# Order of a recurrent stage: transposes in one group, up-projections side by side, feature copies moved to ScalarE

## The chip, the cores and the metric

The kernel runs on one core of one Trainium2 chip. The metric is the device time of one execution, in microseconds; three runs gave 3738.53 us as their median (3736.28 to 3739.94). Five engines work side by side, each through its own list of instructions in a fixed order: TensorE (PE; its weight loads are shown as PEld), VectorE (DVE), ScalarE (ACT), GpSimd (POOL) and SyncE (SP), which issues the DMAs. They meet only at semaphores.

## What is computed

A decoder block over 32 sequences of 256 tokens with 256 features: four sLSTM layers (the first stage), then cross attention and a quantised feed-forward (the second stage, which the change does not touch). One sLSTM layer, cut to what matters:

```python
xc = silu(causal_conv(xn, 4 taps) + cb)             # xn = layernorm(x)
gi, gf = xc @ wi, xc @ wf;  gz, go = xn @ wz, xn @ wo   # per head, 64 x 64
def step(h, c, n, m):                               # 256 tokens, one after another
    ir, fr, zr, og = wx_t + h @ rk + b
    lfm = m + log_sigmoid(fr);  mn = maximum(ir, lfm)
    ig, fg = exp(ir - mn), exp(lfm - mn)
    cn = fg*c + ig*tanh(zr);  nn = fg*n + ig
    hn = sigmoid(og) * cn / nn
x = x + layernorm_per_head(h) * gn_w
x = x + (gelu(u[:336]) * u[336:]) @ wd              # u = layernorm(x) @ wu
```

## The kernel before

The first stage runs 279 steps (`STEPS`). A step handles one token of all 32 sequences in each of the four layers at once: partition group l (32 partitions) holds layer l, six steps behind layer l - 1, so a step is one token through the recurrence, with convolution, norms and feed-forward of neighbouring tokens beside it. Each engine has a loop over j written out by hand in one fixed order; nothing else sets the order.

On TensorE three shapes of the array take turns: full 128x128 transposes (L260, L308), products with 64 rows and 32 columns (`add_bias` L278, `by_head` L269, `centred` L288), and products with 112 or 128 rows and 32 columns (`feed_up` L295, `feed_down` L302). A step goes: transposes of `xm` ("after_cell") and `xn` ("normed"), bias, z and o gates, first half of up, transposes of `h` and `hid`, i and f gates, recurrence, `centred`, `feed_down`, second half of up.

The recurrence closes through the other engines: after the recurrent product (`rec_done`) ScalarE takes Exp and Ln of the f gates (L378, L380), loads another table (L381), and takes tanh of the gates o and z (L383, L384) and of half the decay logit (`td`, L357). VectorE makes `v` (L535), `sf` (L537), and from these the decay logit `dl` (L478: both inputs lie in SBUF), then the cell in four operations (L483, L487, L492, L471) up to `h`, which TensorE transposes. Of VectorE's operations three read both inputs from SBUF: `dl`, the convolved features `xst` (L503) and the residual `xm` (L540). The others read one from PSUM ("banks") or have only one.

GpSimd makes the convolution from `xnt`, the normed features that ScalarE copies out of PSUM (L348): products of taps 2 and 3 in one 128x512 operation (L565), their sum (L571), the products of taps 1 and 0 (L565), the sums that give `part[0]` and `part[1]` (L578, `conv_done`), and the last sum (L579). All of them read SBUF only. ScalarE takes tanh of `part[0]` (`ct`, L365).

Of the kernel before, what the change touches and what calls it, by code (L numbers as in the profile page):

```python
# [14 lines left out]
P = 128  # L15
# [85 lines left out]
def slstm(nc, ctx, a, x4, pieces):  # L101
# [102 lines left out]
    def heads_of(ap, n):  # L204
        return ap.rearrange("p (r n d) -> p n r d", n=HALF, d=DH)[:, n]

    def reach(engine, semaphore, count):
        if count > 0:
            engine.wait_ge(semaphore, count)

# [12 lines left out]
    with nc.Block() as block:  # L223
# [33 lines left out]
        def _(pe):  # L257
# [48 lines left out]
            def hidden_features():  # L306
                for i in range(UTILES):
                    mm = nc.tensor.transpose(bank[0:UT, CV, i * P:(i + 1) * P], hid[:, i * UT:(i + 1) * UT], ident[:])  # L308
                return mm
# [10 lines left out]
            pe.wait_ge(bias_moved, 2 * DMA)  # L320
            add_bias(1).then_inc(first_gates, 1)
# [24 lines left out]
        def _(act):  # L346
            def copy(dst, src):
                return nc.scalar.activation(dst, src, ACT.Copy)  # L348

            def both(ap):  # L350
                return ap.rearrange("p n t -> p (n t)")
# [3 lines left out]
            for j in range(STEPS):  # L355
                act.wait_ge(d_ready, j + 1)
                nc.scalar.activation(td[:], dl[:], ACT.Tanh, scale=-0.5).then_inc(td_done, 1)  # L357
                reach(act, yn_done, j)
                reach(act, rstd_done, j)
                nc.scalar.activation(gl[:], bank[:, UPG, 0:UP], ACT.Gelu, scale=rs2).then_inc(gelu_done, 1)  # L360
                act.wait_ge(xnt_ready, j + 1)
                copy(both(xmt[:]), bank[:, CV, D:]).then_inc(xmt_copied, 1)
                copy(both(xnt[:, j % NRING]), bank[:, CV, 0:D]).then_inc(xnt_copied, 1)
                act.wait_ge(conv_done, j + 1)
                nc.scalar.activation(ct[:], part[:, j % 2, 0], ACT.Tanh).then_inc(ct_done, 1)  # L365
                nc.scalar.preload_act_table_set(LOG_EXP)  # L366
                nc.scalar.activation(spb[:], dl[:], ACT.Exp).then_inc(growth_exp, 1)
                act.wait_ge(growth_exp, j + 1)
                act.wait_ge(h_done, HALF * (j + 1))
                nc.scalar.activation(gate(j - 1, 1), heads(spb[:]), ACT.Ln, bias=1.0).then_inc(growth_log, 1)  # L370
                act.wait_ge(hidt_ready, j + 1)
                copy(both(hidt[:]), bank[0:UT, CV, 0:UTILES * P]).then_inc(hidt_copied, 1)
# [5 lines left out]
                nc.scalar.activation(heads(fb[:]), gate(j, 1), ACT.Exp).then_inc(f_exp, 1)  # L378
                act.wait_ge(f_exp, j + 1)
                nc.scalar.activation(fb[:], fb[:], ACT.Ln, bias=1.0).then_inc(f_log, 1)  # L380
                nc.scalar.preload_act_table(ACT.Gelu)  # L381
                act.wait_ge(sf_done, j + 1)
                nc.scalar.activation(gate(j, 3), gate(j, 3), ACT.Tanh, scale=0.5).then_inc(o_done, 1)  # L383
                nc.scalar.activation(gate(j, 2), gate(j, 2), ACT.Tanh).then_inc(z_done, 1)  # L384
            act.wait_ge(z_done, STEPS)

        @block.vector
        def _(dve):
            n = 0
            for buf, val in ((xr, 0.0), (h, 0.0), (half_r, 0.0), (ls, NEVER), (dl, 0.0), (xm, 0.0), (xst, 0.0), (prod, 0.0), (hid, 0.0),  # L390
                             (hidt, 0.0), (xnt, 0.0), (xmt, 0.0), (gl, 0.0), (xn, 0.0), (v, 0.0), (sf, 0.0), (rstd, 0.0), (eps, EPS), (bias, 0.0), (pick16, 0.0),
# [4 lines left out]
            for l in range(LAYERS):  # L396
                nc.vector.memset(begun[group(l), 0:LAG * l + LEAD + 1], 0.0).then_inc(w_step, 1)
                nc.vector.memset(never[group(l), 0:LAG * l + LEAD + 1], NEVER).then_inc(w_step, 1)
                n += 2
            dve.wait_ge(w_step, n)  # L400
# [69 lines left out]
            def ratio_to_h(j, n):  # L470
                return nc.vector.scalar_tensor_tensor(out=h[:, n * P:(n + 1) * P].rearrange("p (r d) -> p r d", r=2),  # L471
                                                      in0=gates_of(j - 1)[:, :, n, 3, :], scalar=1.0, in1=heads_of(half_r[:], n),
                                                      op0=ALU.add, op1=ALU.mult)

            for j in range(STEPS):
                cell = gate(j - 1, 2)
                reach(dve, sf_done, j)
                nc.vector.scalar_tensor_tensor(out=dl[:], in0=v[:], scalar=-60.0, in1=sf[:], op0=ALU.max,  # L478
                                               op1=ALU.subtract).then_inc(d_ready, 1)
                reach(dve, xm_done, j)  # L480
                nc.vector.bn_stats(stat2[:], xm[:, (j - 1) % MRING]).then_inc(ln2_stat, 1)
                reach(dve, z_done, j)
# [6 lines left out]
                dve.wait_ge(ln2_stat, j + 1)  # L489
# [6 lines left out]
                ratio_to_h(j, 0).then_inc(h_done, 1)  # L496
                dve.wait_ge(gelu_done, j + 1)
                reach(dve, up_done, j)
                nc.vector.scalar_tensor_tensor(out=hid[:], in0=bank[:, UPV, 0:UP], scalar=rs2, in1=gl[:], op0=ALU.mult,
                                               op1=ALU.mult).then_inc(hid_done, 1)  # L500
                ratio_to_h(j, 1).then_inc(h_done, 1)
# [6 lines left out]
                dve.wait_ge(ht_ready, j + 1)  # L508
                nc.vector.tensor_scalar(ht[:].rearrange("p n t -> p (n t)"), bank[:, FD, D:], 1.0 / H_SCALE, None,  # L509
                                        ALU.mult).then_inc(ht_copied, 1)  # L510
# [3 lines left out]
                dve.wait_ge(ln1_stat, j + 1)  # L514
                nc.vector.bn_aggr(mv1, stat1[:]).then_inc(ln1_mv, 1)
                dve.wait_ge(growth_log, j + 1)
                nc.vector.scalar_tensor_tensor(out=heads(sp[:]), in0=gate(j - 1, 1), scalar=40.0, in1=heads(dl[:]), op0=ALU.min,
                                               op1=ALU.max).then_inc(grown, 1)
                dve.wait_ge(grown, j + 1)
                if j < STARTED:  # L520
# [8 lines left out]
                nc.vector.tensor_tensor(yn[:].rearrange("p (r n d) -> p r n d", r=2, n=HALF),  # L529
                                        bank[:, UPG:UPG + 2, UP:UP + P].rearrange("p r (n d) -> p r n d", n=HALF),  # L530
                                        rs.rearrange("p (n r) -> p r n", n=HALF)[:, :, :, None].broadcast_to(
                                            [P, 2, HALF, DH]), ALU.mult).then_inc(yn_done, 1)
                dve.wait_ge(f_exp, j + 1)
                dve.wait_ge(ls_done, j + 1)
                nc.vector.tensor_tensor(heads(v[:]), heads(ls[:]), gate(j, 0), ALU.subtract).then_inc(v_done, 1)  # L535
# [3 lines left out]
                dve.wait_ge(yn_done, j + 1)  # L539
                nc.vector.tensor_tensor(xm[:, j % MRING], yn[:], xr[:, (j - 3) % XRING, :], ALU.add).then_inc(xm_done, 1)  # L540
# [992 lines left out]
```

## Time and profile before

| | us |
|---|---|
| median of three runs | 3738.53 |
| profiled execution | 3732.63 |
| its span (first to last instruction) | 3730.9 |
| PE busy | 3615.0 (97%) |
| DVE busy | 3460.5 (93%) |
| ACT busy | 3064.7 (82%) |
| POOL busy | 2253.7 (60%) |
| mean granted TensorE clock | 0.990 of full speed |

The first stage takes from about 51 us to 2214 us of the span, the second the rest. In a timeline, a row is a run of like instructions: its start, its length from the first start to the last end, and how many. On each engine the next instruction can start somewhat before the one in front has ended, so the difference of two starts is what a row costs its engine, and the length is what somebody has to wait who needs the result.

### The profile page before, as it was taken

Reading aid. Unit: us, or ns where it says so; the run is one execution under the profiler, and the core shown is the slowest. Engines: PE = TensorE matmul, PEld = TensorE weight load, DVE = VectorE, ACT = ScalarE, POOL = GpSimd, SP = SyncE. Lnnn points to the kernel's source line nnn. Section 1 sums busy time; section 2 is a strip of 40 time slices with the busy share of each in tenths; the row PEclk is TensorE's granted clock in tenths of the full one; section 3 lists DMA queues with packets and bytes.
Section 4 is the critical chain, followed back from the end, with each engine's and each line's share of the span. In section 5 each row is a group of like instructions: output and inputs, shape, how many; then the busy total and the mean of one; then the engine's idle time right before and its main releaser. Section 6 shows DMA issues by size and latency. Waiting matters only on the chain. (4 is left out here: it accounts for less than half of the span.)

```text
span 3730.9 us, 167466 instructions
## 1 busy us (share of the span) xinstructions
PE 3615.0 (97%) x71481; PEld 2282.1 (61%) x71481; DVE 3460.5 (93%) x9241; ACT 3064.7 (82%) x6357; POOL 2253.7 (60%) x2395
## 2 busy tenths in 40 slices
PE   6999999999999999999999987999999999999997
PEld 3666666665666666666666654666666666666664
DVE  8999999999999999999999987889988898888886
ACT  4999999999999999999999984677776677777675
POOL 3777777777777777777777764444444444444442
PEclk9999999999999999999999998999999999999998
DMA  2000221000000000000000000000000000100000
GB/s 82 25 25 25 56 59 53 25 25 25 25 25 25 25 25 25 25 25 25 25 25 25 25 26 18 24 24 24 24 24 24 24 24 28 32 24 24 24 16 10
DMA packets 99973, 104.27 MB, mean 28 GB/s; under 512 B 17297, under 2 KB 95005, under 8 KB 98729
## 3 DMA queue, kind: packets, MB, share of 16 engines
q1 hardware_dynamic: 99224, 93.56, 8.7%
q8 instruction: 560, 9.18, 1.0%
q14 instruction: 189, 1.54, 0.1%
HBM read 48.52 MB, written 17.53 MB: 18 GB/s over the span
## 5 line engine op out<-in xcount | busy, mean ns | idle before, releaser
L565 POOL TENSOR_TENSOR conv_products<-normed_features,conv_taps_by_token 128x256 f32<-128x256 f32 (+1 forms) x837 | 757.9, 919 | 530.2 <-ACT normed_features L348 530.1
L771 POOL TENSOR_TENSOR exps_of_both_halves<-scores 128x256 f32<-128x256 f32 x512 | 424.2, 851 | 583.8 <-ACT scores L1027 578.4
L295 PE MATMUL banks<-up_centred,after_cell_features 128*32 128x336 f32 x8928 | 740.3, 449 | 1.1 <-ACT after_cell_features L348 0.5
L295 PEld LDWEIGHTS banks<-up_centred,after_cell_features 128*32 128x32 f32 x8928 | 260.5, 109 | 277.6 <-issue 224.1
L302 PE MATMUL banks<-down,hidden_features 112*32 112x256 f32 x6696 | 419.2, 383 | 0.0
L578 POOL TENSOR_TENSOR conv_partial_sums<-conv_products,conv_partial_sums 128x512 f32<-128x512 f32 x279 | 370.5, 1328 | 21.9
L1027 ACT ACTIVATE scores<-scores 128x512 f32<-128x512 f32 x512 | 305.4, 626 | 77.7 <-DVE scores L1175 74.0
L366 ACT ACT_TABLE_LOAD x279 | 358.0, 1283 | 5.2
L381 ACT ACT_TABLE_LOAD x279 | 358.0, 1283 | 5.1
L1175 DVE SCALAR_TENSOR_TENSOR scores<-banks,score_top 128x512 f32<-128x512 f32 x512 | 327.9, 681 | 26.1 <-PE banks L857 25.5
L269 PE MATMUL banks<-recurrent_weights,h_features 64*32 64x256 f32 x8928 | 313.1, 379 | 0.3 <-DVE h_features L509 0.2
L867 PE MATMUL banks<-scores,v_tokens 128*32 128x256 f32 x4096 | 274.0, 385 | 11.9 <-ACT scores L1027 11.7
L579 POOL TENSOR_TENSOR conv_partial_sums<-conv_products,conv_partial_sums 128x256 f32<-128x256 f32 x279 | 265.1, 950 | 0.0
L302 PEld LDWEIGHTS banks<-down,hidden_features 112*32 112x32 f32 x6696 | 189.0, 109 | 121.3
L571 POOL TENSOR_TENSOR conv_partial_sums<-conv_products,conv_partial_sums 128x256 f32<-128x256 f32 x279 | 220.3, 790 | 65.9 <-DVEq L466 44.0
L835 PE MATMUL banks<-batch_inputs_hi,qkv_weights_hi 128*128 128x256 f16 x1024 | 196.0, 273 | 11.3 <-POOL batch_inputs_lo L759 9.8
L269 PEld LDWEIGHTS banks<-recurrent_weights,h_features 64*32 64x32 f32 x8928 | 196.1, 106 | 8.3 <-DVE h_features L509 1.5
L835 PE MATMUL banks<-batch_inputs_lo,qkv_weights_hi 128*128 128x256 f16 x1024 | 196.0, 273 | 0.0
L835 PE MATMUL banks<-batch_inputs_hi,qkv_weights_lo 128*128 128x256 f16 x1024 | 195.9, 273 | 0.0
L867 PEld LDWEIGHTS banks<-scores,v_tokens 128*32 128x32 f32 x4096 | 120.9, 110 | 107.6 <-ACT scores L1027 27.1
L269 PE MATMUL banks<-gate_weights,convolved_features 64*32 64x128 f32 x8928 | 186.2, 275 | 0.0
L503 DVE SCALAR_TENSOR_TENSOR convolved_features<-tanh_half_conv,conv_partial_sums 128x256 f32<-128x256 f32 x279 | 180.0, 645 | 0.5 <-ACT tanh_half_conv L365 0.5
(222 smaller groups left out, 9933.3 us busy)
## 6 DMA issues: line engine op xcount, KB each, us to landing
layer_inputs<-layer_outputs SPq DMA_DIRECT2D x279, 96.0 KB, 2.0
layer_inputs<-in_x SPq DMA_DIRECT2D x280, 32.0 KB, 1.8
x_scratch<-layer_outputs SPq DMA_DIRECT2D x279, 32.0 KB
x_tokens<-in_x SPq DMA_DIRECT2D x32, 256.0 KB, 3.0
context_features<-in_ctx SPq DMA_DIRECT2D x32, 256.0 KB, 3.7
layers_out<-x_scratch SPq DMA_DIRECT2D x32, 256.0 KB, 2.8
out<-result SPq DMA_DIRECT2D x64, 128.0 KB, 1.8
up_centred<-in_ff_up SPq DMA_DIRECT2D x1, 2688.0 KB
```

What stands on the lines that cost most here:

```text
L269: mm = nc.tensor.matmul(bank[group(l), 2 * (j % 2) + odd, at + g0 * DH:at + g1 * DH], src[r, n, group(l)], w[r, l, n, g0:g1, :].rearrange( ...
L295: mm = nc.tensor.matmul(bank[group(l), b, 0:UP], xmt[:, n, group(l)], up[:, l, n, at:at + UP], start=n == 0, stop=n == HALF - 1, skip_grou ...
L302: mm = nc.tensor.matmul(bank[group(l), FD, 0:D], hidt[:, i, group(l)], down[:, l, i, :], start=i == 0, stop=i == UTILES - 1, skip_group_ch ...
L366: nc.scalar.preload_act_table_set(LOG_EXP)
L381: nc.scalar.preload_act_table(ACT.Gelu)
L565: return nc.gpsimd.tensor_tensor(prod[:, i:i + n], xnt[:, j % NRING].rearrange("p n t -> p (n t)")[:, None, :].broadcast_to([P, n, HALF * ...
L578: nc.gpsimd.tensor_tensor(new[:, 0:2], prod[:, 0:2], old[:, 1:3], ALU.add).then_inc(conv_done, 1)
L771: nc.gpsimd.tensor_tensor(psum[:, i % RING, :], pr[:, i % RING, 0:S], pr[:, i % RING, S:2 * S], ALU.add).then_inc(halves_added, 1)
L835: mm = nc.tensor.matmul(bank[:, b, i * S:(i + 1) * S], w_[:, m, h, (2 * n + i) * P:(2 * n + i + 1) * P], x_[:, j % SLOTS, src, h, :], star ...
L867: mm = nc.tensor.matmul(bank[32 * g:32 * g + 32, b, at:at + S], stationary(kt, i), pr[:, i % RING, kt * S:(kt + 1) * S], start=kt == 0, st ...
L1027: nc.scalar.activation(pr[:, i % RING, :], pr[:, i % RING, :], ACT.Exp, scale=S_SCALE).then_inc(exp_done, 1)
L1175: nc.vector.scalar_tensor_tensor(out=pr[:, i % RING, :].rearrange("p (k s) -> p k s", k=KT), in0=bank[:, i % SCORES, :].rearrange("p (k s) ...
```

## The change

TensorE's step becomes: transposes of `xn`, `h`, `xm` and `hid` together; i and f gates, recurrence, `centred`; `feed_down`, both halves of up; then bias and z and o gates of the next step. The transposed `hid` goes into the i and f places of the gate banks of the step before, and the growth logs, which stood there, into the transposed `h`'s place in the bank of `feed_down`. The copy of the transposed `h` moves from VectorE (L509) to ScalarE, behind the second table load; the copies of `xn` and `xm` and all tanh operations move within ScalarE's step. On VectorE the scaling by the norm and the residual become four 128x64 operations that read PSUM and write `xm`; `sf` now comes ahead of `v`, and `dl` behind the layer's output `xo`. On GpSimd the products of taps 2 and 3 move from the head of a step to behind `conv_done`.

```diff
@@ tensor, in the loop over j
-                reach(pe, xm_done, j)
-                transposes(CV, D, xm[:, (j - 1) % MRING], xmt_ready)
                 transposes(CV, 0, xn, xnt_ready)
-                add_bias(j)
-                by_head(j, wg, xnt[:, (j - 1) % NRING], 2, GATES)
-                pe.wait_ge(xmt_copied, j + 1)
-                feed_up(UPG, 0).then_inc(g_done, 1)
                 pe.wait_ge(h_done, HALF * (j + 1))
                 transposes(FD, D, h, ht_ready)
-                pe.wait_ge(xnt_copied, j + 1)
-                hidden_features().then_inc(hidt_ready, 1)
+                transposes(CV, D, xm[:, (j - 1) % MRING], xmt_ready)
+                pe.wait_ge(hid_done, j + 1)
+                hidden_features(j - 1).then_inc(hidt_ready, 1)
                 ...
+                pe.wait_ge(grown, j + 1)
                 feed_down().then_inc(down_done, 1)
-                pe.wait_ge(yn_done, j + 1)
+                pe.wait_ge(xmt_copied, j + 1)
+                pe.wait_ge(xm_done, j + 1)
+                feed_up(UPG, 0).then_inc(g_done, 1)
                 feed_up(UPV, UP).then_inc(up_done, 1)
+                pe.wait_ge(ls_done, j + 1)
+                add_bias(j + 1)
+                pe.wait_ge(xnt_copied, j + 1)
+                by_head(j + 1, wg, xnt[:, j % NRING], 2, GATES)
@@ scalar, in the loop over j
+                copy(both(ht[:]), bank[:, FD, D:], 1.0 / H_SCALE).then_inc(ht_copied, 1)
...
-                nc.scalar.activation(gate(j - 1, 1), heads(spb[:]), ACT.Ln, bias=1.0).then_inc(growth_log, 1)
+                nc.scalar.activation(bank[:, FD, D:], spb[:], ACT.Ln, bias=1.0).then_inc(growth_log, 1)
@@ vector, in the loop over j
-                nc.vector.tensor_scalar(ht[:].rearrange("p n t -> p (n t)"), bank[:, FD, D:], 1.0 / H_SCALE, None,
-                                        ALU.mult).then_inc(ht_copied, 1)
...
-                nc.vector.tensor_tensor(yn[:].rearrange(...), bank[:, UPG:UPG + 2, UP:UP + P].rearrange(...), rs..., ALU.mult).then_inc(yn_done, 1)
-                nc.vector.tensor_tensor(xm[:, j % MRING], yn[:], xr[:, (j - 3) % XRING, :], ALU.add).then_inc(xm_done, 1)
+                for r in range(2):
+                    for n in range(HALF):
+                        at = slice(r * P + n * DH, r * P + n * DH + DH)
+                        add = nc.vector.scalar_tensor_tensor(out=xm[:, j % MRING, at], in0=bank[:, UPG + r, UP + n * DH:UP + n * DH + DH],
+                                                             scalar=rs[:, 2 * n + r:2 * n + r + 1], in1=xr[:, (j - 3) % XRING, at],
+                                                             op0=ALU.mult, op1=ALU.add)
+                add.then_inc(xm_done, 1)
@@ gpsimd, in the loop over j
-                reach(pool, taps_rest, j)
-                nc.gpsimd.tensor_tensor(new[:, 3], prod[:, 3], new[:, 4], ALU.add).then_inc(sum3_done, 1)
                 reach(pool, xnt_copied, j)
                 reach(pool, conv_done, j)
+                products(0, 1, j - 1).then_inc(taps_first, 1)
                 products(1, 1, j - 1).then_inc(taps_second, 1)
-                products(0, 1, j - 1).then_inc(taps_first, 1)
                 ...
                 nc.gpsimd.tensor_tensor(new[:, 0:2], prod[:, 0:2], old[:, 1:3], ALU.add).then_inc(conv_done, 1)
+                products(2, 2, j - 1).then_inc(taps_rest, 1)
+                pool.wait_ge(taps_rest, j + 1)
+                nc.gpsimd.tensor_tensor(new[:, 3], prod[:, 3], new[:, 4], ALU.add).then_inc(sum3_done, 1)
                 nc.gpsimd.tensor_tensor(new[:, 2], prod[:, 2], old[:, 3], ALU.add).then_inc(sum2_done, 1)
-                pool.wait_ge(xnt_copied, j + 1)
-                pool.wait_ge(sum2_done, j + 1)
-                products(2, 2, j).then_inc(taps_rest, 1)
```

GpSimd's row, one step of the first stage, before; "conv_products" are products with the taps, "conv_partial_sums" the sums of them, and L578 is the one that gives `conv_done`:

```order
L565 TENSOR_TENSOR conv_products<-normed_features,conv_taps_by_token 128x512 [waits sum_of_third_tap,normed_copied]
L571 TENSOR_TENSOR conv_partial_sums<-conv_products,conv_partial_sums 128x256 [waits other_taps_done]
L565 TENSOR_TENSOR conv_products<-normed_features,conv_taps_by_token 128x256 [waits conv_done,normed_copied]
L565 TENSOR_TENSOR conv_products<-normed_features,conv_taps_by_token 128x256
L578 TENSOR_TENSOR conv_partial_sums<-conv_products,conv_partial_sums 128x512 [waits sum_of_third_tap,first_tap_done]
L579 TENSOR_TENSOR conv_partial_sums<-conv_products,conv_partial_sums 128x256
```

The same step after the change, from the wait for ScalarE's copy on (L583 gives `conv_done`):

```order
L572 TENSOR_TENSOR conv_products<-normed_features,conv_taps_by_token 128x256 [waits conv_done,normed_copied]
L572 TENSOR_TENSOR conv_products<-normed_features,conv_taps_by_token 128x256
L583 TENSOR_TENSOR conv_partial_sums<-conv_products,conv_partial_sums 128x512 [waits second_tap_done,sum_of_third_tap]
L572 TENSOR_TENSOR conv_products<-normed_features,conv_taps_by_token 128x512
L586 TENSOR_TENSOR conv_partial_sums<-conv_products,conv_partial_sums 128x256 [waits other_taps_done]
L587 TENSOR_TENSOR conv_partial_sums<-conv_products,conv_partial_sums 128x256
```

The same six operations, but the 128x512 product has gone from first place to fourth.

VectorE's row before, from `sf` (L537) over `dl` (L478) to `h` (L471):

```order
L537 SCALAR_TENSOR_TENSOR softplus_of_minus_f<-softplus_logs,banks 128x256 [waits f_log]
L540 TENSOR_TENSOR after_cell<-cell_out,layer_inputs 128x256 [waits yn_done]
L544 TENSOR_TENSOR layer_outputs<-banks,after_cell 128x256 [waits x4_stored,layer_inputs_moved,down_done]
L478 SCALAR_TENSOR_TENSOR minus_decay_logit<-log_normaliser_minus_i,softplus_of_minus_f 128x256 [waits softplus_done]
L481 BN_STATS bn_stats_ln2<-after_cell 128x6 [waits after_cell_done]
L483 SCALAR_TENSOR_TENSOR banks<-half_cell_ratio,banks 128x4x64 [waits tanh_z_done]
```

And after the change, the same stretch:

```order
L534 SCALAR_TENSOR_TENSOR after_cell<-banks,rstd,layer_inputs 128x64 [waits centred_ready]
L534 SCALAR_TENSOR_TENSOR after_cell<-banks,rstd,layer_inputs 128x64 x3
L539 SCALAR_TENSOR_TENSOR softplus_of_minus_f<-softplus_logs,banks 128x256 [waits f_log]
L542 TENSOR_TENSOR log_normaliser_minus_i<-log_normaliser,banks 128x256 [waits normaliser_done]
L546 TENSOR_TENSOR layer_outputs<-banks,after_cell 128x256 [waits x4_stored,layer_inputs_moved,down_done]
L548 SCALAR_TENSOR_TENSOR minus_decay_logit<-log_normaliser_minus_i,softplus_of_minus_f 128x256 [waits minus_i_done]
L551 BN_STATS bn_stats_ln2<-after_cell 128x6 [waits after_cell_done]
L485 SCALAR_TENSOR_TENSOR banks<-half_cell_ratio,banks 128x4x64 [waits tanh_z_done]
```

`xm` is now written from PSUM in four pieces ahead of `sf`; `dl` (L548) still comes right behind `xo` and ahead of the statistics and of the cell's first operation.

## Rows read from the trace of the kernel before

**Rows 1.** Busy time by engine in a stretch: start:end, length, PE, PEld, DVE, ACT, POOL, clock, DMA share, GB/s.

```profile
1000.00:1400.00 400.00, 399.81 (x10377) 247.84 (x10384) 389.05 (x1187) 378.51 (x826) 294.19 (x310) 1.00 0.10 25
```

**Rows 2.** Timeline of TensorE, one step: start us, length us, engine, line, operation, operands, count.

```profile
1000.02 0.41 PE L278 MATMUL banks<-bias_parts,layer_of_row 64*32 64x512 f16 x8
1000.82 1.34 PE L295 MATMUL banks<-up_centred,after_cell_features 128*32 128x336 f32 x16
1002.08 0.44 PE L260 MATMUL banks<-identity,h 128*128 128x128 f32 x2
...
1007.19 0.44 PE L260 MATMUL banks<-identity,after_cell 128*128 128x128 f32 x2
1007.77 0.41 PE L278 MATMUL banks<-bias_parts,layer_of_row 64*32 64x512 f16 x8
```

**Rows 3.** Timeline of TensorE in a narrow window: the last four of that run of sixteen.

```profile
1001.69 0.47 PE L295 MATMUL banks<-up_centred,after_cell_features 128*32 128x336 f32 x4
```

**Rows 4.** Two VectorE lines over the first stage: duration minimum/median/maximum, first and last start.

```profile
L503 DVE SCALAR_TENSOR_TENSOR convolved_features<-tanh_half_conv,conv_partial_sums x279: 415/664/669, 50.5 to 2212.6; 128x256 f32<-128x256 f32 x140
```
```profile
L540 DVE TENSOR_TENSOR after_cell<-cell_out,layer_inputs x278: 411/418/994, 55.4 to 2208.8; 128x256 f32<-128x256 f32 x139
```

**Rows 5.** Timeline of GpSimd, one step.

```profile
1000.86 1.29 POOL L565 TENSOR_TENSOR conv_products<-normed_features,conv_taps_by_token 128x512 f32<-128x512 f32 x1 [1.87 <-ACT normed_features L348]
...
1002.99 1.42 POOL L565 TENSOR_TENSOR conv_products<-normed_features,conv_taps_by_token 128x256 f32<-128x256 f32 x2
1004.49 1.33 POOL L578 TENSOR_TENSOR conv_partial_sums<-conv_products,conv_partial_sums 128x512 f32<-128x512 f32 x1
1005.78 0.96 POOL L579 TENSOR_TENSOR conv_partial_sums<-conv_products,conv_partial_sums 128x256 f32<-128x256 f32 x1
```

**Rows 6.** Timeline of VectorE, the same step.

```profile
1001.77 0.66 DVE L503 SCALAR_TENSOR_TENSOR convolved_features<-tanh_half_conv,conv_partial_sums 128x256 f32<-128x256 f32 x1
...
1005.73 0.42 DVE L540 TENSOR_TENSOR after_cell<-cell_out,layer_inputs 128x256 f32<-128x256 f32 x1
...
1006.53 0.49 DVE L478 SCALAR_TENSOR_TENSOR minus_decay_logit<-log_normaliser_minus_i,softplus_of_minus_f 128x256 f32<-128x256 f32 x1
1006.95 0.41 DVE L481 BATCH_NORM_STATS2 bn_stats_ln<-after_cell 128x6 f32<-128x256 f32 x1
1007.29 0.40 DVE L483 SCALAR_TENSOR_TENSOR banks<-half_cell_ratio,banks 128x256 f32<-128x256 f32 x1
...
1008.64 0.29 DVE L471 SCALAR_TENSOR_TENSOR h<-banks,half_cell_ratio 128x128 f32<-128x128 f32 x1
```

**Rows 7.** Timelines of GpSimd and VectorE in another step.

```profile
1109.41 1.29 POOL L565 TENSOR_TENSOR conv_products<-normed_features,conv_taps_by_token 128x512 f32<-128x512 f32 x1 [1.88 <-ACT normed_features L348]
```
```profile
1110.56 0.42 DVE L503 SCALAR_TENSOR_TENSOR convolved_features<-tanh_half_conv,conv_partial_sums 128x256 f32<-128x256 f32 x1
```

**Rows 8.** Timeline of ScalarE, from the end of the recurrent product on.

```profile
1004.42 0.38 ACT L378 ACTIVATE softplus_logs<-banks 128x256 f32<-128x256 f32 x1 [0.26 <-PE banks L269]
...
1006.56 0.37 ACT L383 ACTIVATE banks<-banks 128x256 f32<-128x256 f32 x1
1006.84 0.36 ACT L384 ACTIVATE banks<-banks 128x256 f32<-128x256 f32 x1
1007.11 0.42 ACT L357 ACTIVATE tanh_half_d<-minus_decay_logit 128x256 f32<-128x256 f32 x1
1007.41 0.54 ACT L360 ACTIVATE gelu_of_gate<-banks,rstd 128x336 f32<-128x336 f32 x1
...
1008.16 0.38 ACT L348 ACTIVATE normed_features<-banks 128x256 f32<-128x256 f32 x1
1008.42 0.42 ACT L365 ACTIVATE tanh_half_conv<-conv_partial_sums 128x256 f32<-128x256 f32 x1
1008.86 1.28 ACT L366 ACT_TABLE_LOAD   x1
1010.16 0.42 ACT L367 ACTIVATE growth_logs<-minus_decay_logit 128x256 f32<-128x256 f32 x1
```

More of the change, by code:

```diff
@@ L346, in _, with copy @@
         def _(act):
-            def copy(dst, src):
-                return nc.scalar.activation(dst, src, ACT.Copy)
+            def copy(dst, src, scale=1.0):
+                return nc.scalar.activation(dst, src, ACT.Copy, scale=scale)
             def both(ap):
@@ L355, in _ @@
             for j in range(STEPS):
[L356 removed]
+                reach(act, v_done, j)
+                nc.scalar.activation(gate(j - 1, 3), gate(j - 1, 3), ACT.Tanh, scale=0.5).then_inc(o_done, 1)
+                nc.scalar.activation(gate(j - 1, 2), gate(j - 1, 2), ACT.Tanh).then_inc(z_done, 1)
+                reach(act, d_ready, j)
                 nc.scalar.activation(td[:], dl[:], ACT.Tanh, scale=-0.5).then_inc(td_done, 1)
[L358 removed]
+                act.wait_ge(conv_done, j + 1)
+                nc.scalar.activation(ct[:], part[:, j % 2, 0], ACT.Tanh).then_inc(ct_done, 1)
+                reach(act, g_done, j)
                 reach(act, rstd_done, j)
                 nc.scalar.activation(gl[:], bank[:, UPG, 0:UP], ACT.Gelu, scale=rs2).then_inc(gelu_done, 1)
[L361 to L365, printed above, removed]
                 nc.scalar.preload_act_table_set(LOG_EXP)
                 nc.scalar.activation(spb[:], dl[:], ACT.Exp).then_inc(growth_exp, 1)
+                act.wait_ge(ht_ready, j + 1)
+                copy(both(ht[:]), bank[:, FD, D:], 1.0 / H_SCALE).then_inc(ht_copied, 1)
+                act.wait_ge(xmt_ready, j + 1)
+                copy(both(xnt[:, j % NRING]), bank[:, CV, 0:D]).then_inc(xnt_copied, 1)
                 act.wait_ge(growth_exp, j + 1)
[L369 to L370 removed]
+                act.wait_ge(ht_copied, j + 1)
+                nc.scalar.activation(bank[:, FD, D:], spb[:], ACT.Ln, bias=1.0).then_inc(growth_log, 1)
                 act.wait_ge(hidt_ready, j + 1)
[L372 removed]
+                copy(hidt[:], hidden_of(j - 1)).then_inc(hidt_copied, 1)
+                act.wait_ge(gn_stat, HALF * (j + 1))
                 act.wait_ge(ln1_mv, j + 1)
@@ L378, in _ @@
                 nc.scalar.activation(heads(fb[:]), gate(j, 1), ACT.Exp).then_inc(f_exp, 1)
+                copy(both(xmt[:]), bank[:, CV, D:]).then_inc(xmt_copied, 1)
                 act.wait_ge(f_exp, j + 1)
@@ L399, in _ @@
                 n += 2
+            nc.vector.bn_stats(stat2[:], xm[:, 0]).then_inc(w_step, 1)
+            n += 1
             dve.wait_ge(w_step, n)
@@ L468, in _ @@
             dve.wait_ge(first_x, DMA)
[L470 to L473, printed above, removed]
             for j in range(STEPS):
                 cell = gate(j - 1, 2)
[L477 to L482, printed above, removed]
+                dve.wait_ge(z_done, j + 1)
                 nc.vector.scalar_tensor_tensor(out=cell, in0=heads(half_r[:]), scalar=-2.0 / H_SCALE, in1=cell, op0=ALU.mult,
@@ L495, in _ @@
                 dve.wait_ge(ratio_done, j + 1)
-                ratio_to_h(j, 0).then_inc(h_done, 1)
+                for n in range(HALF):
+                    nc.vector.scalar_tensor_tensor(out=h[:, n * P:(n + 1) * P].rearrange("p (r d) -> p r d", r=2),
+                                                   in0=gates_of(j - 1)[:, :, n, 3, :], scalar=1.0, in1=heads_of(half_r[:], n),
+                                                   op0=ALU.add, op1=ALU.mult).then_inc(h_done, 1)
+                reach(dve, up_done, j)
                 dve.wait_ge(gelu_done, j + 1)
-                reach(dve, up_done, j)
                 nc.vector.scalar_tensor_tensor(out=hid[:], in0=bank[:, UPV, 0:UP], scalar=rs2, in1=gl[:], op0=ALU.mult,
                                                op1=ALU.mult).then_inc(hid_done, 1)
-                ratio_to_h(j, 1).then_inc(h_done, 1)
                 dve.wait_ge(ct_done, j + 1)
@@ L528, in _ @@
                 dve.wait_ge(cen_ready, j + 1)
[L529 to L535, printed above, removed]
+                for r in range(2):
+                    for n in range(HALF):
+                        at = slice(r * P + n * DH, r * P + n * DH + DH)
[3 more added lines that the diff above has]
+                add.then_inc(xm_done, 1)
                 dve.wait_ge(f_log, j + 1)
```

42 lines of the change are left out of this document (25 added, 17 removed).

## The prediction

> **What bounds the kernel now.** First I look at the busy time by engine in a stretch of the first stage [rows 1]: of 400 us TensorE is busy 399.8, VectorE 389, ScalarE 378.5, GpSimd 294. All of the first three are nearly full, so the order of waits decides as much as the work. Next TensorE's timeline [rows 2]: from bias to bias 7.75 us pass, and no row there shows idle time. Its transposes do not wait for their inputs: those of xm start at 1007.19, and xm was finished at 1006.15 [rows 2, 6]. What they wait for is the array: the transposes of h start 0.39 us after the last four up matmuls, while four such matmuls inside the run take 0.29 (0.87 us for the first twelve) [rows 2, 3]. So the step before is TensorE's own loop of 7.75 us. By the first and last start of one line the first stage lies between 50.5 and 2212.6 us [rows 4]: 2162.1 over 278 steps is 7.777 a step, so outside this loop there are only 0.025 a step, 7 us in all. The second stage is the same code before and after; I add nothing for it.
>
> **A stall that has no row of its own.** The third view is the duration of VectorE's operations that have both inputs in SBUF. The convolved features, L503, take 664 ns in the middle and 415 at the least [rows 4]. The timelines show why. The slow one starts at 1001.77 with GpSimd's 128x512 product running until 1002.15 (1000.86 + 1.29), and ends at 1002.43, 0.28 behind the product's end [rows 5, 6]. In the step where only 0.14 us of the product are left (it ends at 1110.70), L503 starting at 1110.56 takes 0.42 [rows 7]. The decay logit dl, L478, does the same: it starts at 1006.53, GpSimd's L579 ends at 1006.74, and dl ends at 1007.02, again 0.28 later [rows 5, 6]. L540 starts 0.09 ahead of L578's end and takes 0.42. One rule fits all: such an operation, started while GpSimd works, ends at its own 0.41 or at GpSimd's end plus 0.28, whichever is later. Before the change this hits xst, where TensorE has other work, and dl by 0.08. The question is where it hits afterwards.
>
> The Trainium skill (SBUF — State Buffer, Who interferes with whom) says that a VectorE instruction with two SBUF inputs contends with a GpSimd instruction that reads SBUF, and that the later one blocks fully. The trace agrees that it waits for the whole GpSimd instruction, but not that all its work is still ahead of it then: 0.28 us follow, not 0.41. By the page the sum below would be 0.13 us a step higher, 36 us in all.
>
> **The change part by part.**
>
> TensorE: the products and transposes are as many as before. Of six switches between shapes of the array four are left, and a switch costs what the end of the up run costs over its inside, 0.39 - 0.29 = 0.10 us [rows 2, 3]. So the loop falls by 0.2 us to 7.55; ends of 0 (the neighbours now behind one another don't overlap better) and 0.4 (each twice as dear).
>
> VectorE loses the copy of h and two 128x256 operations and gets four of 128x64. No row has that form: each costs between 0.10 and the 0.29 of a 128x128 one [rows 6], I take 0.14. They stand ahead of sf, which waits for ScalarE's Ln and hides them at 0.14; at 0.29 each they would start dl some 0.4 later, which the paragraph on dl shows to be free too (it has 0.73). xst becomes free of the stall, since in its new place GpSimd is idle; TensorE comes to the i and f gates later than xst ends either way, so that is worth nothing in the ring below.
>
> ScalarE gets one more 0.38 us copy, of h; it counts in the ring below. The copy of xm goes between Exp and Ln of f: Ln then starts two starts of 0.28 behind Exp instead of 0.38 and a latency, 0.15 later, which counts in the first rival only.
>
> The added waits on TensorE: feed_down waits for the growth, and both halves of up, bias and gates are queued behind it. With E as the end of dl (below), the growth's Ln follows the copy of xn at about E + 3.4 and the growth is done at E + 4.2, feed_down is reached past E + 5; the wait is covered by 0.8 us, and without that cover would cost one for one. The transposes of hid wait for hid, E + 2.6, and are reached at E + 2.7, a cover of 0.1. SyncE's DMAs hang on xo, which keeps its place behind feed_down.
>
> GpSimd: the products of taps 2 and 3 move from the front of its step to behind conv_done. That is the edit on which the sum rests. GpSimd's step starts when ScalarE has copied the normed features; call that moment C. I follow from rows: 0.07 to the first product (the copy at 1008.16 ends 1008.54, the product one step on from 1000.86 starts at 1008.61), 1.50 for two products and the pause behind them (1002.99 to 1004.49), 1.29 for the conv sum (1004.49 to 1005.78) [rows 5, 8]. So the 128x512 product starts at C + 2.86 and runs to C + 4.15.
>
> Now dl. Let E be its end. The chain behind it on VectorE: the statistics start 0.07 ahead of E (1006.95 against 1007.02), the cell's first operation 0.34 later, h's first half 1.35 after that, the second 0.21 later (0.29 less the overlap of 0.08), its end 0.29 on, and 0.04 to TensorE: E + 2.16 [rows 6]. From there to Exp of f, which waits for the recurrent product, 2.34 us pass before (1002.08 to 1004.42) [rows 2, 8]; the transposes of xm are now between, 0.27, so Exp of f is at E + 4.77. dl comes 2.11 behind Exp of f (1006.53 against 1004.42) and still will: xo ahead of it waits for feed_down, and those runs follow the recurrent product as before. So dl is ready to start at E + 6.88.
>
> And C: ScalarE takes td 0.04 after E (ends 0 and 0.09, what lies between dl's end and td now), then ct 0.30 later and Gelu 0.31 later (a 0.42 us tanh holds the engine 0.30: 1007.11 to 1007.41), the table load 0.56 later (0.54 and 0.02, as between ct and its load), Exp of the growth 1.29 later (1008.86 to 1010.16), the copy of h 0.30 later, that of xn 0.28 later (as from o to z), and 0.38 for it [rows 8]. Sum: 3.46. So C = E + 3.46, the product runs from E + 6.32 to E + 7.61, and dl, ready at E + 6.88, comes 0.56 behind its start and 0.73 ahead of its end. By the rule dl ends at E + 7.61 + 0.28 = E + 7.89.
>
> This is a ring: dl, td, ct, Gelu, table load, copies, four GpSimd operations, dl. It closes at **7.89 us** a step, and it feeds itself, since a later dl moves the copy and with it the product that blocks the next dl. Nothing on it is waited for from elsewhere: the transposed h is there at E + 2.65 (2.16, 0.44 and a latency) and wanted at E + 2.80; conv_done comes at C + 2.9, which is ahead of E, and ct asks behind E. TensorE's loop of 7.55 has 0.34 of idle time inside it.
>
> Sum: 7.89 - 7.75 = 0.14 us a step, times 279: +39 us. Against this L540, which by its maximum of 994 ns was sometimes blocked for a whole GpSimd operation more [rows 4], becomes an operation that reads PSUM; of the 7 us beyond the loop I take half as due to it, 4 us (ends 0 and 7). +35 us. Own time of the profiled execution 3732.6 (span 3730.9): 3768. The runs' median lies 5.9 above that execution: **3774 us**.
>
> **The rivals.**
>
> *The stall does not reach dl, and the change pays* (0.12). If the rule is another (say, only behind this product's own start of step), TensorE's 7.55 loop bounds. The second loop is shorter: from Exp of f to o 2.14 and the 0.15 above, z and its end 0.28 + 0.36 [rows 8], the cell 0.04 + 1.35 + 0.21 + 0.29 + 0.04, and 2.61 to the next Exp of f: 7.47. That is -0.20 a step, -56 us: 3683. For it: fewer switches. Against it: three kinds of VectorE operation obey the rule, and one of them is dl itself. The Trainium skill (TensorEngine Tiling (Array Packing), Key Properties) says that a change of tiling mode drains the array, which speaks for the gain on TensorE; the rows give 0.10 for one such change.
>
> *dl does all its work behind the product* (0.06): where it started long before the product's end, its own 0.41 would follow instead of 0.28. The ring becomes 8.02, +0.13 a step, 36 us more: 3810. For it speaks only that no row shows dl behind this very product; against it that L503 does the same behind it with 0.28 [rows 5, 6]. The Trainium skill's rule above (SBUF — State Buffer, Who interferes with whom) is this rival.
>
> *No change* (0.06): the product is over when dl comes, or nearly. The ring then must be 0.14 shorter than I add up, some seven of its terms 0.02 too long, or dl later by 0.6. Time 3735.
>
> *Slower by much* (0.02): dl loses against the next sum too, as L540 sometimes did, by 0.994 - 0.418 = 0.58 more a step [rows 4]: +161 us, 3935. Behind the product the next sum waits for it, so VectorE comes first.
>
> **How the numbers follow.** The forecast has 0.74. Its own range: the latencies (0.04 down, 0.05 up) and the overlaps, 0.07 us in all, is 20 us either way, 3754 to 3794. The range takes in a little on the side of no change and nearly all of the second rival: 3748 to 3808. Left out are the gain (0.12), the large loss (0.02) and some edges. What can be told from no change here is 0.2%, 7.5 us. Slower has 0.74 + 0.06 + 0.02 = 0.82, the same 0.06, faster 0.12.
>
> **What would show it.** In the profile of the changed kernel L548 (dl) should take about 1.0 us (7.89 - 6.88) and end 0.28 behind the 128x512 product of L572; L507 (xst) about 0.42. ScalarE should wait for dl ahead of td, some 0.3 us a step, and TensorE for h ahead of its transposes, about as much; TensorE's busy share in the first stage falls by a few per cent. If dl takes 0.41 to 0.5 and TensorE never waits, the first rival holds. If ScalarE waits for the transposed h, the ring I add up isn't the one that closes.

## The result, and the profile after

The changed kernel takes 3776.32 us in the median of four runs (3774.36 to 3777.15) against 3737.69 before: a ratio of 1.0102, with an interval of 1.0085 to 1.012. It is slower, as forecast, and 3776 stands against 3774. The span of the profiled execution grows from 3730.9 to 3775.4 us. One execution of experiment 3 took 8926.32 us, with the matmuls of the up projection at 1019 ns in the mean against 448 (experiment 8); no comparison uses it, and why it was slow is not known.

Two lines over the first stage of the changed kernel, dl and xst (duration minimum/median/maximum in ns, first and last start):

```profile
L548 DVE SCALAR_TENSOR_TENSOR minus_decay_logit<-log_normaliser_minus_i,softplus_of_minus_f x279: 415/1050/1068, 57.3 to 2258.9; 128x256 f32<-128x256 f32 x140
```
```profile
L507 DVE SCALAR_TENSOR_TENSOR convolved_features<-tanh_half_conv,conv_partial_sums x279: 411/414/856, 50.7 to 2254.5; 128x256 f32<-128x256 f32 x140
```

The stall has changed places: xst has gone from 664 to 414 ns, dl from 0.49 us [rows 4, 6] to 1.05. From 50.7 to 2254.5 are 2203.8 us against 2162.1, so 41.7 of the 44.5 us lie in the first stage.

GpSimd's timeline of the changed kernel, and VectorE's and ScalarE's beside it, answer to [rows 5, 6, 8]:

```profile
1004.59 1.43 POOL L572 TENSOR_TENSOR conv_products<-normed_features,conv_taps_by_token 128x256 f32<-128x256 f32 x2 [2.26 <-ACT normed_features L355]
1006.16 1.28 POOL L583 TENSOR_TENSOR conv_partial_sums<-conv_products,conv_partial_sums 128x512 f32<-128x512 f32 x1
1007.41 1.28 POOL L572 TENSOR_TENSOR conv_products<-normed_features,conv_taps_by_token 128x512 f32<-128x512 f32 x1
```
```profile
1005.66 0.51 DVE L528 TENSOR_SCALAR normed<-layer_inputs,moments,rstd 128x256 f32<-128x256 f32 x1
1006.11 0.86 DVE L534 SCALAR_TENSOR_TENSOR after_cell<-banks,rstd,layer_inputs 128x64 f32<-128x64 f32 x4
...
1007.91 1.06 DVE L548 SCALAR_TENSOR_TENSOR minus_decay_logit<-log_normaliser_minus_i,softplus_of_minus_f 128x256 f32<-128x256 f32 x1
```
```profile
1001.08 0.42 ACT L367 ACTIVATE tanh_half_d<-minus_decay_logit 128x256 f32<-128x256 f32 x1 [0.28 <-DVE minus_decay_logit L548]
1001.40 0.40 ACT L369 ACTIVATE tanh_half_conv<-conv_partial_sums 128x256 f32<-128x256 f32 x1
1001.71 0.52 ACT L372 ACTIVATE gelu_of_gate<-banks,rstd 128x336 f32<-128x336 f32 x1
1002.25 1.28 ACT L373 ACT_TABLE_LOAD   x1
1003.55 0.42 ACT L374 ACTIVATE growth_logs<-minus_decay_logit 128x256 f32<-128x256 f32 x1
1003.87 0.36 ACT L355 ACTIVATE h_features<-banks 128x256 f32<-128x256 f32 x1
1004.13 0.37 ACT L355 ACTIVATE normed_features<-banks 128x256 f32<-128x256 f32 x1
...
1009.00 0.42 ACT L367 ACTIVATE tanh_half_d<-minus_decay_logit 128x256 f32<-128x256 f32 x1 [0.29 <-DVE minus_decay_logit L548]
```

The whole ring stands here. td starts at 1001.08; the copy of xn ends at 1004.50; GpSimd's products start 0.09 later, the sum at 1006.16, the 128x512 product at 1007.41, until 1008.69. dl has started 0.50 behind that product and ends at 1008.97, 0.28 behind its end. td follows at 1009.00, 7.92 us after the one before.

Who waited for whom in 400 us of the changed kernel (us in total, times, longest):

```profile
PEld banks L264 <- DVE h L499: 22.4, 51, 0.5
ACT tanh_half_d L367 <- DVE minus_decay_logit L548: 14.4, 51, 0.3
```

Both once a step, 0.44 and 0.28 us. TensorE's busy time in such a stretch falls from 399.8 us [rows 1] to 389.7:

```profile
1000.00:1400.00 400.00, 389.70 (x10127) 246.92 (x10119) 391.82 (x1212) 372.39 (x859) 274.42 (x303) 1.00 0.09 25
```

### The profile page after: what moved, and what is told of

Same layout as the page of the kernel before. It is cut to its first block and busy times, and to the rows that moved or that the text cites. A ratio compares the mean times of both kernels' runs of the same rounds, so it can differ in the third digit from the quotient of the medians.

```text
span 3775.4 us, 168598 instructions
## 1 busy us (share of the span) xinstructions
PE 3605.5 (95%) x71489; PEld 2312.7 (61%) x71489; DVE 3514.7 (93%) x9520; ACT 3072.2 (81%) x6636; POOL 2180.0 (58%) x2395
## 5 line engine op out<-in xcount | busy, mean ns | idle before, releaser
L299 PE MATMUL banks<-up_centred,after_cell_features 128*32 128x336 f32 x8928 | 682.7, 446 | 0.0
L299 PEld LDWEIGHTS banks<-up_centred,after_cell_features 128*32 128x32 f32 x8928 | 293.2, 109 | 301.0 <-issue 248.3
L583 POOL TENSOR_TENSOR conv_partial_sums<-conv_products,conv_partial_sums 128x512 f32<-128x512 f32 x279 | 359.0, 1287 | 39.9
L548 DVE SCALAR_TENSOR_TENSOR minus_decay_logit<-log_normaliser_minus_i,softplus_of_minus_f 128x256 f32<-128x256 f32 x279 | 290.8, 1042 | 0.0
L534 DVE SCALAR_TENSOR_TENSOR after_cell<-banks,rstd,layer_inputs 128x64 f32<-128x64 f32 x1116 | 239.9, 278 | 1.8 <-PE banks L292 1.4
L586 POOL TENSOR_TENSOR conv_partial_sums<-conv_products,conv_partial_sums 128x256 f32<-128x256 f32 x279 | 222.1, 796 | 21.9
L587 POOL TENSOR_TENSOR conv_partial_sums<-conv_products,conv_partial_sums 128x256 f32<-128x256 f32 x279 | 203.1, 728 | 0.0
```

What stands on the lines that cost most here:

```text
L299: mm = nc.tensor.matmul(bank[group(l), b, 0:UP], xmt[:, n, group(l)], up[:, l, n, at:at + UP], start=n == 0, stop=n == HALF - 1, skip_grou ...
L583: nc.gpsimd.tensor_tensor(new[:, 0:2], prod[:, 0:2], old[:, 1:3], ALU.add).then_inc(conv_done, 1)
```

## Experiments

Each ratio is to the kernel before on the same chip: 3733.68 us for experiments 1 to 4, 3736.81 for 5, 7 and 8, 3731.92 for 9 and 10. "The changed kernel" is the 3776 us above; it did not run again on these chips, so differences to it, and between experiments of different chips, are uncertain by some 6 us. "The middle step" is the median distance of two starts of `L528` (`L526` in the kernel before), "the mean step" the distance of its first and last start over 278. Number 6, sf in PSUM in the kernel before, gave no measurement.

**1. dl reads one input from PSUM.** Edits: sf is written behind `down_done` to the free half of `feed_down`'s bank, in the order v, statistics, sf, xo, dl; ScalarE's tanh of the gate o waits for sf instead of v.

```diff
-                nc.vector.scalar_tensor_tensor(out=heads(sf[:]), ...).then_inc(sf_done, 1)
+                dve.wait_ge(down_done, j + 1)
+                nc.vector.scalar_tensor_tensor(out=heads(bank[:, FD, D:]), ...).then_inc(sf_done, 1)
 ...
-                nc.vector.scalar_tensor_tensor(out=dl[:], in0=v[:], scalar=-60.0, in1=sf[:], op0=ALU.max,
+                nc.vector.scalar_tensor_tensor(out=dl[:], in0=v[:], scalar=-60.0, in1=bank[:, FD, D:], op0=ALU.max,
```

> The changed kernel, with sf written to the free half of feed_down's bank (PSUM) instead of SBUF, so that dl reads only one input from SBUF; sf waits for feed_down, so sf, xo, dl follow in this order and v and the statistics come ahead. Theory (the ring through GpSimd, 7.92 us a step): dl takes 0.41 instead of 1.05 whatever GpSimd does, the ring is open, and TensorE's loop of about 7.55 bounds: 0.37 x 279 = 103 us less than the changed kernel, about 3675, under the kernel before too. Rival (the step is long because TensorE's new order or ScalarE's extra copy is, and dl only fills idle time): no gain, 3770 to 3780.

Measured: 3688.13 us, ratio 0.9876 (0.9861 to 0.9891). dl takes 409 ns at the median and 416 at most, with GpSimd's order as in the changed kernel. It runs inside the 128x512 product and is not blocked:

```profile
1006.70 1.29 POOL L573 TENSOR_TENSOR conv_products<-normed_features,conv_taps_by_token 128x512 f32<-128x512 f32 x1
```
```profile
1007.48 0.41 DVE L551 SCALAR_TENSOR_TENSOR minus_decay_logit<-log_normaliser_minus_i,banks 128x256 f32<-128x256 f32 x1
```

The step is 7.54 us in the middle, as expected, but 7.61 in the mean, and the time 13 us above the expected 3675. `L528` takes up to 1526 ns in this run; experiments 5 and 10 ask how much of the loss is due to it.

**2. The product waits for dl.** The cleanest test: one wait on the engine that has idle time.

```diff
+                reach(pool, d_ready, j)
                 products(2, 2, j - 1).then_inc(taps_rest, 1)
```

> The changed kernel, with one wait more on GpSimd: the 128x512 product starts only when dl is done. No operation, place or operand of another engine is changed. Theory: dl takes 0.41; the three GpSimd operations behind it then run until about 2.9 us after dl, so that xst is blocked for some 0.25 us and TensorE waits about 0.1 for it: 7.55 to 7.65 a step, 3675 to 3702. Rival (GpSimd's work is what is long, or GpSimd is idle 2.3 us a step and so cannot matter): the same as the changed kernel, or slower by the delay of its sums.

Measured: 3671.14 us, ratio 0.9828 (0.9811 to 0.9844). dl in its timeline lines:

```profile
L548 DVE SCALAR_TENSOR_TENSOR minus_decay_logit<-log_normaliser_minus_i,softplus_of_minus_f x279: 406/415/418, 56.9 to 2156.2; 128x256 f32<-128x256 f32 x140
```

A wait added to GpSimd takes 105 us off the changed kernel, and no operation was changed. The four executions spread more than elsewhere (3660.02 to 3674.11). The middle step is 7.47, below the 7.55 to 7.65 expected, and the time is below the 3675 to 3702: TensorE's loop was put too long, and xst takes 463 ns at the median, 0.05 more than in the changed kernel where 0.25 was expected.

**3. The copies swapped.**

```diff
-                act.wait_ge(ht_ready, j + 1)
-                copy(both(ht[:]), bank[:, FD, D:], 1.0 / H_SCALE).then_inc(ht_copied, 1)
                 act.wait_ge(xmt_ready, j + 1)
                 copy(both(xnt[:, j % NRING]), bank[:, CV, 0:D]).then_inc(xnt_copied, 1)
+                act.wait_ge(ht_ready, j + 1)
+                copy(both(ht[:]), bank[:, FD, D:], 1.0 / H_SCALE).then_inc(ht_copied, 1)
```

> The changed kernel with the two copies on ScalarE swapped: that of xn ahead of that of h. Theory: the copy of xn lies on the ring and ends 0.26 us earlier, so the product and with it dl's end come 0.26 earlier: 7.66 a step, 73 us less, about 3704; the copy of h ends 0.26 later, just when TensorE gets to the recurrent product. Rival (the ring closes through the transposed h, whose copy gates the recurrence): 0 to 0.26 longer a step, 3776 to 3850.

Measured: 3948.69 to 3950.65 us in four executions, ratio 1.0578 (1.0561 to 1.0596). Neither theory holds. Experiment 8 is the look at it.

**4. The ring made longer.**

```diff
-                nc.gpsimd.tensor_tensor(new[:, 0:2], prod[:, 0:2], old[:, 1:3], ALU.add).then_inc(conv_done, 1)
+                nc.gpsimd.tensor_tensor(new[:, 1], prod[:, 1], old[:, 2], ALU.add)
+                nc.gpsimd.tensor_tensor(new[:, 0], prod[:, 0], old[:, 1], ALU.add).then_inc(conv_done, 1)
```

> The changed kernel with GpSimd's 128x512 sum that gives conv_done done as two sums of 128x256. Theory: it lies on the ring and takes about 0.76 + 0.73 instead of 1.25, 0.24 more, so a step takes 8.16: 67 us more, about 3843. Rival (GpSimd is idle 2.3 us a step): the 0.24 disappear in that idle time, 3776.

Measured: 3813.86 us, ratio 1.0216 (1.02 to 1.0231), 38 us above the changed kernel. The direction is the ring's, the size 0.14 a step instead of 0.24, because my term was too large: it added lengths where the distance of starts counts. GpSimd's timeline here:

```profile
1006.69 0.74 POOL L583 TENSOR_TENSOR conv_partial_sums<-conv_products,conv_partial_sums 128x256 f32<-128x256 f32 x1
1007.38 0.75 POOL L584 TENSOR_TENSOR conv_partial_sums<-conv_products,conv_partial_sums 128x256 f32<-128x256 f32 x1
1008.08 1.29 POOL L572 TENSOR_TENSOR conv_products<-normed_features,conv_taps_by_token 128x512 f32<-128x512 f32 x1
```

The two sums take 1.39 (1006.69 to 1008.08) where one took 1.25; the middle step is 8.06, so all 0.14 arrive, through an engine idle over 2 us a step.

**5. The sum waits for xn**, added to experiment 2.

```diff
@@ against experiment 2
                 pool.wait_ge(taps_second, j + 1)
+                reach(pool, xn_done, j)
                 nc.gpsimd.tensor_tensor(new[:, 0:2], prod[:, 0:2], old[:, 1:3], ALU.add).then_inc(conv_done, 1)
```

> The second experiment (128x512 product behind dl) with one wait more on GpSimd: the sum that gives conv_done starts only when xn is written. In that experiment 278 steps take 7.467 us in the middle but 7.557 in the mean; in its long steps (8.70) the operation that writes xn (L528, one input and one output in SBUF) takes 1.42 us instead of 0.50, after a DMA came late. Theory of the long steps: L528 too is blocked by GpSimd, and when it starts as late as the sum it loses against the whole sum. With the wait it can't, the long steps of 8.7 go (those that wait for the DMA stay, at most 0.3 longer) and the mean falls to 7.48 to 7.50: 3650 to 3657, against 3671. Rival (the long steps are due to the late DMA alone, L528 is only slow in them): no gain, 3671 or more by the wait.

Measured: 3658.28 us, ratio 0.9792 (0.9775 to 0.9808), the fastest kernel here and just above the 3650 to 3657 expected. What the wait removes is seen in experiment 2, in a long step, GpSimd and VectorE:

```profile
1190.09 1.28 POOL L583 TENSOR_TENSOR conv_partial_sums<-conv_products,conv_partial_sums 128x512 f32<-128x512 f32 x1
```
```profile
1190.11 1.42 DVE L528 TENSOR_SCALAR normed<-layer_inputs,moments,rstd 128x256 f32<-128x256 f32 x1
```

L528 ends at 1191.53, 0.16 behind the sum's end. With the wait it takes 511 ns at most:

```profile
L528 DVE TENSOR_SCALAR normed<-layer_inputs,moments,rstd x279: 405/501/511, 54.1 to 2139.1; 128x256 f32<-128x256 f32 x140
```

The mean step falls from 7.555 to 7.500, and TensorE is busy throughout:

```profile
1000.00:1400.00 400.00, 399.95 (x10782) 264.12 (x10769) 386.92 (x1287) 389.39 (x912) 290.23 (x322) 1.00 0.10 26
```

The late DMAs remain (8.9 us of VectorE's waits in the stage, against 0.7 in the changed kernel): with shorter steps the layer outputs' DMA is at times not back in time.

**7. GpSimd's order undone alone.** The 128x512 product and its sum stand first in a step again, ahead of the other products.

> The changed kernel with GpSimd's order undone alone: the 128x512 product and its sum come first again in a step, ahead of the products of taps 1 and 0 and of conv_done. Theory of rings: conv_done now comes 5.05 us behind the copy of xn (0.08 + 1.36 + 0.78 + 1.50 + 1.33) and ct waits for it; from ct to the next copy's end are 3.10 us, so the ring is 8.2 us a step: 78 us more than the changed kernel, 3854 (3840 to 3870). dl takes some 0.5 us only. Rival (the move of the product is what made the change slow, undoing it gives the gain of TensorE's order): 3670 to 3700. Rival (GpSimd has idle time enough): 3776.

Measured: 3841.30 us, ratio 1.0281 (1.0265 to 1.0296), a middle step of 8.15 where 8.2 was added up. ScalarE's timeline:

```profile
1005.68 0.42 ACT L367 ACTIVATE tanh_half_d<-minus_decay_logit 128x256 f32<-128x256 f32 x1
1006.82 0.42 ACT L369 ACTIVATE tanh_half_conv<-conv_partial_sums 128x256 f32<-128x256 f32 x1 [0.72 <-POOL conv_partial_sums L586]
```

ct waits 0.72 us for the sum, while td, ahead of it, waits for nothing. (dl takes 607 ns at the median, some 0.5 us was expected; it is not on this ring.) So with ct moved ahead of Gelu the product has to stand behind conv_done; only, it must also let dl pass.

**8. Experiment 3 once more, for its profile.**

> The third experiment once more, for a profile in which TensorE has its usual speed. It took 3950 instead of the 3704 that the ring through the copies gives: 0.62 us a step more than the changed kernel. Theory now: with the copy 0.26 earlier GpSimd's products end before xn is due, L528 starts beside the following sum and is blocked for all of it, 1.3 to 1.45 us in each step instead of 0.50; everything behind it, dl too, comes so much later. Rival (the copy of h, now second, gates the recurrent product): L528 stays at 0.50, and TensorE waits for ScalarE ahead of its recurrent products by 0.6 us.

Measured: 3952.78 us, in one execution. VectorE, GpSimd and ScalarE:

```profile
1004.41 1.45 DVE L528 TENSOR_SCALAR normed<-layer_inputs,moments,rstd 128x256 f32<-128x256 f32 x1
...
1007.55 0.53 DVE L548 SCALAR_TENSOR_TENSOR minus_decay_logit<-log_normaliser_minus_i,softplus_of_minus_f 128x256 f32<-128x256 f32 x1
```
```profile
1002.87 1.42 POOL L572 TENSOR_TENSOR conv_products<-normed_features,conv_taps_by_token 128x256 f32<-128x256 f32 x2 [2.73 <-ACT normed_features L355]
1004.43 1.28 POOL L583 TENSOR_TENSOR conv_partial_sums<-conv_products,conv_partial_sums 128x512 f32<-128x512 f32 x1
...
1007.07 0.73 POOL L586 TENSOR_TENSOR conv_partial_sums<-conv_products,conv_partial_sums 128x256 f32<-128x256 f32 x1
```
```profile
1007.32 0.37 ACT L364 ACTIVATE banks<-banks 128x256 f32<-128x256 f32 x1 [0.74 <-DVE log_normaliser_minus_i L542]
```

The theory written for this run holds: L528 is blocked for the whole sum in each step and ends at 1005.86, 0.15 behind it; what follows on VectorE is late, and ScalarE waits 0.74 for v. The ring now runs through L528 and closes at 8.54 us. dl is still on it: it starts at 1007.55 within GpSimd's next sum (1007.07 to 1007.80) and ends at 1008.08, 0.28 behind that sum's end, and td follows at 1008.12. But of the 8.54 us dl's stall is only 0.12; L528 takes 0.95 more than its 0.50.

**9. The control in the kernel before.** Its last sum waits for dl.

```diff
+                pool.wait_ge(d_ready, j + 1)
                 nc.gpsimd.tensor_tensor(new[:, 2], prod[:, 2], old[:, 3], ALU.add).then_inc(sum2_done, 1)
```

> The kernel before the change, with one wait more on GpSimd: its last sum of a step (L579) starts only when dl is done. GpSimd stands idle there anyway, so it costs nothing, and dl takes 0.41 instead of 0.49; xm (L540) no longer meets a second sum behind the first. Theory: before the change TensorE's own loop bounds and the stall of dl lies in its cover, so the time stays within 0.2% of the kernel before, at most 5 us less for the few steps in which xm took 0.99: ratio 0.998 to 1.001. Rival (a stall costs what it lasts wherever it is): 0.08 x 279 and those 5 us, 27 us less: ratio 0.993.

Measured: 3729.38 against 3731.92 us, ratio 0.9993 (0.9984 to 1.0002). dl takes 415 ns at the median:

```profile
L478 DVE SCALAR_TENSOR_TENSOR minus_decay_logit<-log_normaliser_minus_i,softplus_of_minus_f x279: 406/415/426, 46.7 to 2210.2; 128x256 f32<-128x256 f32 x140
```

It changes nothing that is clear of noise: in TensorE's cover the stall was free, and the rival's 0.993 lies outside the interval.

**10. Experiment 1 with the wait of experiment 5.**

> The first experiment (sf in feed_down's bank) with the wait of the fifth: the sum that gives conv_done starts only when xn is written. Theory: the first experiment's 7.537 in the middle and 7.612 in the mean differ by the steps in which L528 meets the whole sum (8.95); they go, and the mean falls to 7.55 or 7.56: 3688 less 15 to 17, about 3672. Rival (the long steps come from the late DMA alone): 3688.

Measured: 3678.51 us, ratio 0.9855 (0.984 to 0.987). That is 10 us less than experiment 1 where 15 to 17 were expected, and 8 by the ratios on each chip, whose intervals overlap. L528 stays under 0.52 us, but the mean step falls only from 7.61 to 7.59 and not to 7.55, so in this order L528 explains the smaller part of the long steps. VectorE waits for the late DMA (11.4 us in the stage, up to 1.1 at once); that this is the rest was not shown. xo stands one operation later in this order, and its DMA with it, which fits; that link was not tried by itself.

## Why the prediction was right

*The mechanism.* The ring dl, td, ct, Gelu, load, copies, GpSimd, dl is shown: opened at dl by the operand (1) and by the time (2) it vanishes, lengthened by 0.14 it gives 0.14 (4). All marks that were named are in the profile: dl at 1.05 (1.0 said), 0.28 behind the product, xst at 0.41, ScalarE waiting 0.28 (0.3 said), TensorE 0.44 ahead of the transposes of h (0.34 by the sum). In the kernel before, where no ring through dl bounds, taking its stall away gave nothing (9).

*The sum.* 7.92 us a step against 7.89: two products with their pause took 1.57 instead of 1.50 and the sum behind them 1.25 instead of 1.29, the rest is round-off. That is +8 us. The irregular steps nearly vanished (mean 7.924 to a middle 7.917 in the starts of L528), about -5 instead of -4, and some 3 us lie outside the first stage. 39 + 8 - 5 + 3 is, but for round-off, the 44.5 of the spans.

*Luck.* That 3776 stands against 3774 flatters the sum. It said +35 us; the spans of the two profiled executions differ by 44.5, the medians by 38.6. The forecast took the profiled execution's 3732.6 and added the 5.9 by which the median lay above it; in the changed kernel the profiled execution is 0.8 above the median. And of the terms on GpSimd one was 0.07 too small and one 0.04 too large, which partly cancel.

*Terms that were off and cost nothing.* The four 128x64 operations take 276 ns each and 0.2 between starts, not 0.14. TensorE's loop is 7.47, not 7.55 (experiments 2 and 5, where its matmuls have next to no idle time). TensorE in experiment 2, and below it two rows of the kernel before that [rows 2] leave out:

```profile
1000.21 0.44 PE L264 MATMUL banks<-identity,normed 128*128 128x128 f32 x2
...
1001.34 0.67 PE L273 MATMUL banks<-gate_weights,convolved_features 64*32 64x128 f32 x32
...
1004.50 2.45 PE L299 MATMUL banks<-up_centred,after_cell_features 128*32 128x336 f32 x32
1006.88 0.41 PE L282 MATMUL banks<-bias_parts,layer_of_row 64*32 64x512 f16 x8
```
```profile
1002.78 0.67 PE L269 MATMUL banks<-gate_weights,convolved_features 64*32 64x128 f32 x32
...
1005.94 1.31 PE L295 MATMUL banks<-up_centred,after_cell_features 128*32 128x336 f32 x16
```

All transposes together take 1.13 (1000.21 to 1001.34) instead of the 1.28 of the two groups before, the two up halves side by side 2.38 instead of 2.51. That is the whole 0.28 us a step by which TensorE's loop got shorter, where the sum had 0.2 for two switches. It is worth 78 us, and experiment 5 is 78.5 us under the kernel before; the changed kernel gave all of it away at one operation of VectorE.

*What was wrong.* "One rule fits all", for operations with both inputs in SBUF, left one out: L528, with one input and one output in SBUF, is blocked too. In the changed kernel it takes 0.51 and ends 0.15 behind the products (1006.02 to 1006.17), off the path. It made experiment 3 miss and accounts for most of what the long steps of experiment 2 cost, and for some of it in experiment 1. The trace of the kernel before had it already, six times at more than 0.9 us, as L526:

```profile
L526 DVE TENSOR_SCALAR normed<-layer_inputs,moments,rstd x279: 405/407/1456, 53.5 to 2215.1; 128x256 f32<-128x256 f32 x140
```

The section on the change has a slip as well: the transposed hid goes to the z and o places of the gate bank, not i and f.

*The rivals.* The first (stall not at dl) is refuted by dl's 1.05 us; its price was nearly right once the stall is taken away (3683 said, 3658 to 3688 measured). That dl does all its work behind the product is refuted by the 0.28, no change by the interval, and the loss against the next sum too by dl's longest 1.07 us.

*Open.* In experiment 8 L528's recorded start is 0.02 ahead of the sum's and it still loses. The traces together say more: L528 (L526 before) lost against a GpSimd operation in all 263 cases in which that started 0.013 to 0.094 us behind it, and won in all cases from 0.102 us on. L540 in the kernel before goes by the recorded starts alone: it won when the next sum started from 0.027 us behind it on (0.05 in [rows 5, 6]), and lost seven times when it had started 0.016 to 0.043 us ahead. Why the two kinds differ was not found. sf in PSUM in the kernel before was not measured.

## What to carry to other kernels

Where VectorE and GpSimd share a loop, give each VectorE operation that can block (both inputs in SBUF, or a tensor_scalar from SBUF to SBUF) a window in which no long GpSimd operation runs: a wait on the idle engine may be worth more than the work it delays. A stall moves with the order; ask not how long it is but whether a ring closes through it. After such a change add up every ring that crosses the two engines, with idle engines included.

## What the runs showed of the hardware

- A VectorE operation of 128x256 with two SBUF inputs that starts within a GpSimd one with more than 0.15 us left ends 0.276 to 0.288 us behind its end, in all 2469 such cases of the traces (0.41 if never blocked): L503, L507, L540, L478, L548. The GpSimd operation is not longer for it (the 128x512 product takes 1.29 at the median beside dl and 1.29 without). With one input in PSUM dl is not blocked (0.416 at most, experiment 1).
- L528, a tensor_scalar from SBUF to SBUF, ends 0.14 to 0.16 behind it, and takes 0.405 if never blocked. The Trainium skill (SBUF — State Buffer, Who interferes with whom) names tensor_scalar among those that can enter a two-port mode and contend. The rows above agree that it contends; whether it ran in such a mode no run here shows.
- GpSimd's sums are blocked in turn: the 128x256 one took 0.96 in the kernel before, beside xm [rows 5, 6], and 0.73 when it waited for dl and ran alone (experiment 9).
